# A 16-row, two-layer post-norm transformer in one kernel: first mixture and small attention one step earlier in the loop, routing at step 2, reciprocal roots of gathered rows once a group

## What is computed

```python
x = layernorm(x + attn0(x))   # RMS norm, 16 heads of 64, softmax over 256 keys
x = layernorm(x + moe0(x))    # router with bias, top 2 of 8 experts (128-256-128, gelu) + a shared expert
x = layernorm(x + attn1(x))   # per token: softmax over 16 "heads" of size 8, then a projection
x = layernorm(x + moe1(x))    # router, top 2 of 8 experts (128-512-128, gelu)
```

## Time and profile before

| | us |
|---|---|
| median of 3 runs | 1513.58 |
| lowest and highest run | 1510.7, 1517.77 |
| the profiled execution, its own time | 1511.41 |
| its span, first to last instruction | 1509.7 |

### The profile page before, as it was taken

How to read it: one execution, slowest core, us unless ns; L and a number is a source line. 1 busy time by engine, 2 the same in 40 slices (tenths; PEclk the granted TensorE clock), 3 DMA queues, 4 the chain that set the end, 5 groups by cost and what they waited for, 6 DMA issues and landing times.

```text
span 1509.7 us, 27533 instructions
## 1 busy us (share of the span) xinstructions
PE 1223.3 (81%) x9532; PEld 1040.3 (69%) x9532; DVE 942.9 (62%) x2405; ACT 833.6 (55%) x2405; POOL 579.5 (38%) x504
## 2 busy tenths in 40 slices
PE   6898969887978787878788887868787869999805
PEld 5776758675867676757575767657676748999805
DVE  4466676767766676766766767675776665721235
ACT  5775647565656565655656574645565554654401
POOL 3015151606060606151525242245646360513564
PEclk9998999899999999999989998999999988999957
DMA  4110000000000000000000000000000013999813
GB/s 137 76 69 5 1 5 2 4 1 5 1 5 1 1 5 1 5 1 5 1 5 1 5 1 5 1 5 29 4 22 2 22 38 123 339 337 349 274 35 106
DMA packets 50875, 76.64 MB, mean 51 GB/s; under 512 B 6058, under 2 KB 36147, under 8 KB 50739
## 3 DMA queue, kind: packets, MB, share of 16 engines
q1 hardware_dynamic: 46898, 67.02, 13.1%
q0 software_dynamic: 3840, 7.87, 1.7%
HBM read 58.75 MB, written 16.12 MB: 50 GB/s over the span
## 4 chain that ended last, share of the span: by engine, by line
issue 37%; DVE 17%; POOL 16%; ACT 13%; PE 11%; DVEq 3%; POOLq 2%; DMA 1%; SPq 0%; ACTq 0%
ACT probs L758 7%; POOL prod_buffer L645 5%; POOL values L671 3%; DVE score L1156 2%; DVEq L437 2%; POOL xs L660 2%; POOLq L437 2%; DVE neg_max L912 2%; POOL std_inv L601 2%; ACT probsT L737 2%; DVE score L1161 2%; DVE shifted L967 2%; PE bank_S L1398 2%; DVE x L956 1%; DVE prod_buffer L1131 1%
## 5 line engine op out<-in xcount | busy, mean ns | idle before, releaser
L758 ACT ACTIVATE probs<-bank_S,neg_max 128x256 f32<-128x256 f32 x512 | 235.9, 475 | 141.1 <-DVE neg_max L912 141.1
L912 DVE TENSOR_REDUCE neg_max<-bank_S 128x2 f32<-128x512 f32 x256 | 164.6, 684 | 112.4 <-PE bank_S L1398 111.2
L645 POOL TENSOR_TENSOR prod_buffer<-score,qkv 128x1024 f32<-128x1024 f32 x60 | 167.7, 2818 | 51.2 <-ACT score L774 51.2
L633 POOL TENSOR_TENSOR prod_buffer<-qkv 128x1024 f32<-128x1024 f32 x45 | 124.1, 2758 | 140.9 <-ACT qkv L737 140.9
L1457 PE MATMUL bank_A<-probsT,values 128*64 128x256 f32 x1024 | 150.1, 417 | 4.5 <-ACT probsT L737 3.2
L600 POOL TENSOR_TENSOR var_eps<-mv,ln_eps 128x2 f32<-128x2 f32 x48 | 9.5, 198 | 364.1 <-DVE mv L950 364.1
L1435 PE MATMUL bank_T<-ident,probs 128*128 128x128 f32 x1024 | 145.3, 285 | 1.8 <-ACT probs L758 0.6
L737 ACT ACTIVATE probsT<-bank_T 128x512 f32<-128x512 f32 x256 | 139.4, 604 | 8.8 <-PE bank_T L1435 8.8
L1435 PEld LDWEIGHTS bank_T<-ident,probs 128*128 128x128 f32 x1024 | 117.2, 145 | 36.9 <-issue 30.8
L1549 PE MATMUL bank_F<-down,hid 128*128 128x128 f32 x960 | 119.5, 281 | 4.5 <-DVE x L1014 3.5
L1549 PEld LDWEIGHTS bank_F<-down,hid 128*128 128x128 f32 x960 | 114.9, 198 | 7.9 <-DVE x L1014 6.5
(11 more groups left out here) (333 smaller groups left out, 3370.9 us busy)
## 6 DMA issues: line engine op xcount, KB each, us to landing
probs<-in_w SPq DMA_DIRECT2D x22, 512.0 KB, 5.4
oT<-in_w SPq DMA_DIRECT2D x21, 512.0 KB, 4.8
w_own<-in_w SPq DMA_DIRECT2D x19, 512.0 KB, 5.4
probsT<-in_w SPq DMA_DIRECT2D x11, 512.0 KB, 5.1
xb<-xs SPq DMA_DIRECT2D x36, 128.0 KB, 5.5
wo<-in_w SPq DMA_DIRECT2D x9, 512.0 KB, 5.6
xs<-hid SPq DMA_DIRECT2D x36, 128.0 KB, 5.5
xs<-w_own SPq DMA_DIRECT2D x1, 3072.0 KB, 9.6
```

The lines of the kernel that those rows point to most:

```text
L633: settled(pool, g.tensor_tensor(prod[:, t, half(i)], q, k, ALU.mult))
L645: g.tensor_tensor(pv1[:, t, half(i)], *weights_and_values(t, i), ALU.mult).then_inc(pv1_ready, 1)
L758: ins = sc.activation(probs[:, h // 2 % 2, h % 2, t, :], unit.bank(f"S{h}")[:, t * S:(t + 1) * S], ACT.Exp, bias=neg_max[:, h, t:t + 1], a ...
L912: ve.tensor_reduce(neg_max[:, h, :], v.bank(f"S{h}")[:, :].rearrange("p (t k) -> p t k", t=NT), AX.X, ALU.max, negate=True).then_inc(max_r ...
```

## The change

Four things are moved in the loop, and one in the tail. (1) The units of the first mixture, of the small attention and of the second routing stand one step or more earlier in PE's order; ACT's and DVE's parts follow: `mix(1)` and `mix(2)` in step 0, `mix(3)` and `first_out` in step 1, `ln_apply(1)` in step 2, the copies of LQ and `head_product` in step 3. `head_scores` and `head_exp` stay. (2) `second_norm` is in step 0, the copy of X3T in step 1, `second_route` in step 2; `map_blocks` and `input_norm` go to step 4. (3) QK0 takes a bank of the ring G instead of A, and `first_pair(1)` stands behind `first_route`. (4) `inverse_out` takes a group of rows: POOL gathers a group without roots between, waits for the statistics of the row whose buffer it takes, and makes the roots once for rows 0 to 9, once for rows 10 to 14, once for row 15; DVE applies them at the end of a group, for group 1 after the last `dense_mix` and the statistics of row 15.

```diff
--- before.py
+++ after.py
@@ -99,9 +99,9 @@
     return len([q for q in range(min(p + 1, SPARSE)) if q % RING == p % RING])
 
 
-FILL_B = {(0, 1): ["D0p2"], (1, 0): ["WT0"], (1, 1): ["D0p3"], (2, 0): ["D0base"], (3, 0): ["X2T"], (4, 0): ["LQ0", "LQ1"]}
-FILL_C = {(2, 1): ["X3T"], (5, 1): ["R1"]}
-FILL_MAP = {(2, 1): ["CN"]}
+FILL_B = {(0, 0): ["D0p2"], (0, 1): ["WT0", "D0p3"], (1, 1): ["D0base"], (2, 1): ["X2T"], (3, 0): ["LQ0", "LQ1"]}
+FILL_C = {(1, 0): ["X3T"], (2, 0): ["R1"]}
+FILL_MAP = {(3, 1): ["CN"]}
 BESIDE = {0: ["X3T"], 1: ["R1"], 2: ["RK"], 3: ["X2T"], 4: ["CN", "LQ0", "LQ1"], 13: ["AOT"], 14: ["PROJ"], 16: ["X3E"], 17: ["R1E"]}
 EXPS, GATE_EXPS = 8, (4, 19)
 
@@ -149,7 +149,7 @@
         put("A", "HT", on=nxt and s == HP - 2)
         put("F", *fill_units(it, s, 1))
     put("A", f"O{HP - 1}")
-    put("A", "QK0", on=nxt)
+    put("G", "QK0", on=nxt)
     put("G", "OUT")
     put("G", "RK", on=it >= 2)
     put("G", "V0", "V1", "V2", "V3", on=nxt)
@@ -671,11 +671,12 @@
                         g.indirect_dma_start(yg[:, row % YG_RING, t, c, :], None, xs[i].rearrange("b s d -> (b s) d"),
                                              bass.IndirectOffsetOnAxis(ap=slots_of[:, row, t, c:c + 1], axis=0)).then_inc(gathered[row % YG_RING], 16)
 
-            def inverse_out(row):
-
-                pool.wait_ge(out_stats_ready, row + 1)
-                settled(pool, g.tensor_tensor(var_out[:, row, :], mv_out[:, row, :, 1], ln_eps[:], ALU.add))
-                g.tensor_tensor(std_out[:, row, :], var_out[:, row, :], minus_half[:], ALU.pow).then_inc(out_std_ready, 1)
+            def inverse_out(rows):
+
+                pool.wait_ge(out_stats_ready, rows[-1] + 1)
+                whole = slice(rows[0], rows[-1] + 1)
+                settled(pool, g.tensor_tensor(var_out[:, whole, :], mv_out[:, whole, :, 1], ln_eps[:].rearrange("p (a t) -> p a t", a=1).broadcast_to([P, len(rows), NT]), ALU.add))
+                g.tensor_tensor(std_out[:, whole, :], var_out[:, whole, :], minus_half[:].rearrange("p (a t) -> p a t", a=1).broadcast_to([P, len(rows), NT]), ALU.pow).then_inc(out_std_ready, 1)
 
             def tail(v):
                 inverse_std(v, 1, 1)
@@ -683,12 +684,13 @@
                 for row in GROUPS[1]:
                     scatter(row)
                 inverse_std(v, 2, 1)
-                for row in range(ROWS - 1):
-                    gather(row)
-                    if row >= 2:
-                        inverse_out(row - 2)
-                for row in range(ROWS - 3, ROWS):
-                    inverse_out(row)
+                for rows in GROUPS:
+                    for row in rows:
+                        if row >= YG_RING:
+                            pool.wait_ge(out_stats_ready, row - YG_RING + 1)
+                        gather(row)
+                    inverse_out(rows)
+                inverse_out(range(ROWS - 1, ROWS))
 
             def body(v):
                 if v.it == ROWS:
@@ -854,23 +856,23 @@
                         transposed_probs(v, s)
                     if v.a and s + 1 < HP:
                         softmax_exp(v, 2 * s + 2)
-                    if v.b and s == 3:
-                        copy_out(v, "X2T", x2T[:], v.bank("X2T")[:, 0:S])
                     if v.a and s + 1 < HP:
                         softmax_exp(v, 2 * s + 3)
                     if v.a and s >= 1 and s != HP - 2:
                         o_out(v, s - 1)
+                    if v.b and s == 3:
+                        for t in range(NT):
+                            copy_out(v, f"LQ{t}", qkv1[:, t].rearrange("p h c d -> p (h c d)"), v.bank(f"LQ{t}")[:, 0:3 * D])
                     if v.a and s != HP - 2:
                         repeat_inverse(v, s)
-                    if v.b and s == 1:
+                    if v.b and s == 0:
                         copy_out(v, "WT0", gates0T, v.bank("WT0")[0:E + 1, 0:S])
                     if v.a and s != HP - 2:
                         transposed_probs(v, s)
                     if v.a and s + 3 < HP:
                         qk_out(v, s + 3)
-                    if v.b and s == 4:
-                        for t in range(NT):
-                            copy_out(v, f"LQ{t}", qkv1[:, t].rearrange("p h c d -> p (h c d)"), v.bank(f"LQ{t}")[:, 0:3 * D])
+                    if v.b and s == 2:
+                        copy_out(v, "X2T", x2T[:], v.bank("X2T")[:, 0:S])
                     if v.next and s == 1:
                         squares_of(v)
                     if v.b and s == 5:
@@ -1099,7 +1101,7 @@
                 dve.drain()
 
             def out_norm(row):
-                dve.wait_ge(out_std_ready, row + 1)
+                dve.wait_ge(out_std_ready, group_of(row) + 1 if row < ROWS - 1 else len(GROUPS) + 1)
                 for t in range(NT):
                     ins = ve.tensor_scalar(x3[:, row, t, :], x3[:, row, t, :], mv_out[:, row, t, 0:1], std_out[:, row, t:t + 1],
                                            ALU.subtract, ALU.mult)
@@ -1245,21 +1247,17 @@
                 second_gate(row)
                 for r in GROUPS[0]:
                     combine(r)
-                    if r >= 2:
-                        out_norm(r - 2)
-                for r in GROUPS[0][-2:]:
+                for r in GROUPS[0]:
                     out_norm(r)
                 dense_mix(v, 0)
                 dense_mix(v, 1)
                 for n, r in enumerate(GROUPS[1]):
                     dense_mix(v, n + 2)
                     combine(r)
-                    if n >= 2:
-                        out_norm(r - 2)
                 dense_mix(v, E - 1)
-                for r in GROUPS[1][-2:]:
+                out_stats(row)
+                for r in GROUPS[1]:
                     out_norm(r)
-                out_stats(row)
                 out_norm(row)
 
             def body(v):
@@ -1271,41 +1269,40 @@
                     mix(v, 0, False)
                 inverse_sums(v, 0)
                 for s in range(HP):
-                    if v.b and s == 3:
-                        ln_apply(1, x2[:], v.at(1, 1, 1))
                     if s + 1 < HP:
                         head_max(v, 2 * s + 2)
                         head_max(v, 2 * s + 3)
                     if s + 2 < HP:
                         lower_qk(v, s + 2)
                     if v.b and s == 0:
-                        mix(v, 1, False)
+                        mix(v, 1)
+                        mix(v, 2, False)
                     if v.b and s == 1:
-                        mix(v, 2, False)
-                    if v.b and s == 2:
                         mix(v, 3)
                     if s >= 1:
                         o_scale(v, s - 1)
+                    if v.c and s == 0:
+                        second_norm(v.it - 2)
+                    if v.c and s == 1:
+                        transposed_out(v, "X3T", x3T[:])
                     if v.b and s == 2:
-                        first_out(v)
+                        ln_apply(1, x2[:], v.at(1, 1, 1))
                     if s + 1 < HP:
                         inverse_sums(v, s + 1)
-                    if v.c and s == 1:
-                        second_norm(v.it - 2)
-                    if s == 2 and v.it in MAP_ITERATION:
+                    if v.b and s == 1:
+                        first_out(v)
+                    if v.b and s == 3:
+                        head_product(v)
+                    if v.c and s == 2:
+                        second_route(v, "R1", v.it - 2)
+                    if s == 4 and v.it in MAP_ITERATION:
                         map_blocks(v)
-                    if v.c and s == 3:
-                        transposed_out(v, "X3T", x3T[:])
-                    if v.next and s == 3:
+                    if v.next and s == 4:
                         input_norm(v)
                     if v.next and s == HP - 2:
                         input_transposed(v)
-                    if v.b and s == 4:
-                        head_product(v)
                     if v.b and s == 5:
                         head_scores(v, 0)
-                    if v.c and s == HP - 2:
-                        second_route(v, "R1", v.it - 2)
                     if v.b and s == HP - 1:
                         head_scores(v, 1)
                 o_scale(v, HP - 1)
@@ -1320,12 +1317,12 @@
                     place_row(v, v.it - 2)
                 ln_apply(0, x1[:], v.at(0, 1, 1))
                 transposed_out(v, "X1T", None, x1T)
-                if v.next:
-                    first_pair(v, 1)
                 if v.b:
                     head_softmax_sum(v, 0)
                     head_out(v, 0)
                 first_route(v)
+                if v.next:
+                    first_pair(v, 1)
                 if v.b:
                     head_softmax_sum(v, 1)
                     head_out(v, 1)
```

## The result

The changed kernel takes **1490.97 us** (median of 4 runs, 1490.47 to 1491.35) against 1514.04 us of the kernel before in the same session (4 runs, 1510.7 to 1517.77): ratio 0.9847, 95% interval 0.9823 to 0.987. So it is faster by 1.5%, and the forecast of 1443 us with its range of 1420 to 1480 us is missed by 48 us.

What follows compares the result with a forecast made beforehand. No engine is full; chains of waits set the end. From the profiled 1511.4 us, loop -36 and tail -35, plus 2.2 to the median of the runs: 1442.6, rounded to 1443 us, range 1420 to 1480.

Steps and rivals of the forecast that it cites:

- loop sum: Loop: -4.1 + 1.5 at head_scores(1), ln_apply(0) 2.4 us earlier; -36 us over 15 iterations.
- net cost at the input transpose: Loop, end of the earlier mixture's lateness: 1.5 us late, bounds 0 (all given back) and 2.9 (nothing).
- Part 3: Loop, small attention earlier: POOL's head products start about 4 us earlier; input_norm beside them waits 1.1 us, bounds 0 and 2.8.
- Part 2: Loop, mixture one step forward: step-1 scores 2.9 us late, partly given back after step 3, net cost 1.5 us.
- Part 1: Loop, second_route moved from step 6 to step 2 on DVE: gain of 4.1 us before o_scale(6).
- the hole: Loop, DVE's stretch from the end of hT_lo to o_scale(6), holding second_route: 4.1 us, longer than the work.
- Part 4: Loop end, QK0 into ring G: OUT follows o_scale(6) on PE, takes 3.6 to 4.57 us; gain 0.3, bounds 0 and 1.0.
- Part 5: Tail, grouped roots on POOL: gathers at 5.08 us a row, first root pair 3.0 us; gain 35 us, bounds 28 and 38.
- (a): Rival: loop gives nothing, lateness and held input_norm use up second_route's gain; only the tail gains, 1478.6 us; chance 0.20.
- (c): Rival: tail gathers stay at 7.5 us a row, the DMA queue's pace; tail gives some 10 us, 1467.6 us; chance 0.10.
- (d): Rival: step 0's order delays step 1, nothing given back; loop loses 4.8 us an iteration, 1550.6 us; chance 0.05.
- What would show it: Signs in loop and tail: 76 us between residuals, gathers every 5.1 us; a 78 us period or 7.5 us pitch refutes.

Runs made afterwards that it cites:

- e5_both: Changed kernel with input_norm ahead of POOL's head products and POOL's first product waiting for both LQ copies: 1524.99 us against 1567.81 of the kernel before, ratio 0.9729.
- e7_oldtail: Kernel of e5_both, but with the tail of the kernel before: 1465.06 us where the kernel before takes 1515.11, ratio 0.9667.
- e9_late: Kernel of e5_both with only the second routing put back to step 6, behind the input transpose: 1451.24 us against 1515.11 of the kernel before, ratio 0.9571.
- cured loop: Loop of e5_both, the changed loop with both edits against held DVE instructions: 75.1 us between residuals, where the changed loop has 79.2.
- a2_after: The changed kernel itself, run again on another chip where the kernel before takes 1567.81 us: 1586.81 us, ratio 1.0134.
- e5c_both: Same kernel as e5_both, run once more where the kernel before takes 1569.17 us: 1527.08 us, ratio 0.9762.
- the first run: The changed kernel as first timed and profiled: 1490.97 us against 1514.04 of the kernel before, ratio 0.9847.

## Why the prediction was wrong

The forecast's execution was 1511.4 - 36 - 35 = 1440.4 us, the profiled one took 1490.5: 50 us apart. The part ahead of the tail accounts for 36 + 8.5 = 44.5 of them, the tail for 35 - 29.5 = 5.5. The term of the loop sum that failed is the net cost at the input transpose: 1.5 us within bounds of 0 and 2.9, measured 5.0. With it the gain of 4.1 us is gone. Two instructions that POOL holds make the difference; without them the cost is 0.9.

- **Part 3 is the step that failed.** It foresaw the collision of `input_norm` with POOL's products and priced it at 1.1 us within bounds of 2.8; it is 3.53 - 0.47 = 3.05 us. Its argument was that the wait ends with one POOL product and that the next `head_max` has slack for a part; in the trace the two instructions wait for a sum and then a product, and the `head_max` follows without a gap. The Trainium skill (SBUF — State Buffer, § Who interferes with whom), which Part 3 set aside as not shown, says that a `tensor_scalar` in a two-port mode and a GpSimd instruction shut each other out for a whole instruction; here the first of the two starts at 666.31 and 1.2 us later POOL's sum of 666.17 ends (667.45), the second ends with the product of 667.41 (669.76), and the trace agrees. The second collision was not foreseen at all: Part 2 put DVE's `head_product` "into a place where DVE waits anyhow", at no cost. It is held for 3.27 - 1.23 = 2.04 us. In the earlier trace rows DVE had begun it at 655.60, 0.05 us ahead of POOL's at 655.65, and POOL had paid (3.39 us). In the changed order ACT's copy of LQ0 lets POOL go before DVE is free. The same section of the Trainium skill says that the one that issues first gets the ports; 3.27 and 2.36 us in the one order, 1.23 and 3.18 in the other (e5_both) agree. Together 5.1 us, each directly ahead of a `head_max`: the +4.8 us of iteration 1. Without them the mean over all 15 iterations is 75.4 us (e7_oldtail) where 76.0 was forecast.
- **Part 1** was right that `shifted` was held and that the hole had 4.1 us, and wrong in whom it credited. e9_late gives the routing's own move 0.8 us an iteration. The effects of the two moves don't add up: with the small attention earlier the collision is gone, with the routing in step 2 and in step 6 alike. The sum also counted 15 iterations, and iteration 1 has no second routing and no hole.
- **Part 2's** 2.9 us (3.3 measured) at step 1 was right. That half of it is given back by the input transpose was wrong in the changed kernel, but right, even too careful, in the cured loop, with 0.9 us left.
- **Part 4**: OUT takes 3.73 us at a granted clock of 1.00 (684.2 to 687.9), as its lower bound of 3.6 said. The working missed that OUT waits for `o_scale(6)` and `o_scale(7)` only in front of its last matmuls; it begins at 684.23, 0.7 us ahead of the end of `o_scale(7)`. That changed no sign.
- **Part 5** had the right mechanism. Gathers at 5.06 us a row against 5.08; row 9's statistics 55.3 us behind the first gather against 55.5; norms 5.21 against 5.6. Mis-sized is the root pair: 7.2 us and not 3.0. That it is nearly the upper bound is luck: the bound was ten times the power of 2 columns, and the power takes 3.55 us, the drain ahead of it 3.42 though nothing is in flight. The second pair, 1.78 + 1.99 us, had no term; `dense_mix(7)` and the statistics of row 15, 1.6 us in the sum, run beside it, and so does row 15's own root beside the norms. The 4.2 us of the first pair and about 2 of the second, with small gains elsewhere, make the 5.5.
- **The rivals.** (a), the loop gives nothing, was the nearest with 1478.6, and its reason names `input_norm` held; it lacked the head product and thus a loss. (c) is refuted, the gathers keep their pace. (d) came true for iteration 1 alone, and by another mechanism; that its 4.8 us are met to the digit is chance. That the tail could turn against the kernel on another chip stood nowhere.
- **What would show it** expected `input_norm` over 0.5 us, `shifted` near 0.2 and the step-1 scores 2 to 3 us late, and all came; so none of them tells the forecast from a loss. The period of 78 us, its sign of being wrong, came too: 79.2.

## What to carry to other kernels

When work of one engine moves beside a long instruction of another that can hold it, here DVE's beside POOL's, list every instruction in the new neighbourhood and ask who starts first; a two-input instruction that was harmless by 0.05 us is a term of the sum. A cure by order (one more wait on POOL, one call moved up) was worth more here than the change itself: 1586.8 us became 1525.0 on one chip. A gain from taking waits out of a queue of DMAs should be measured on more than one chip: here the waits were what let the other engines go on.

## What the runs showed that was not expected

- **A drain on POOL has a price for each indirect DMA issued since the last one, even when all have landed**: 0.15 us behind none, 0.47 behind 4, 1.14 behind 12, 1.47 behind 16, 1.78 behind 20, 3.42 behind 40, so 0.15 us and about 0.08 for each. Behind 4 gathers just issued it is 1.6 to 4.7 us in the kernel before.
- **A power on POOL costs by the column**: 0.70 us for 2, 1.99 for 10, 3.55 for 20, so about 0.16 us a column beyond a fixed 0.4. The plain addition ahead of it takes 0.20 to 0.21 us for any of them.
- **Indirect DMAs in a row can slow the other engines to a crawl.** On one kind of chip 40 of them without a drain left 52 GB/s and 3 matmuls in 10 us. In a2_after PE's records stand 2.8 us apart, each put down to no wait that the profile shows:

```profile
1462.26 0.37 PE L1531 MATMUL bank_S<-probs,hidb 128*128 128x128 f32 x1 [2.44 <-issue]
1465.06 0.37 PE L1531 MATMUL bank_S<-probs,hidb 128*128 128x128 f32 x1 [2.43 <-issue]
```

  DVE too stands still between instructions of one routine (e5c_both), which follow each other without a gap in the first run:

```profile
1400.96 0.61 DVE L1091 SCALAR_TENSOR_TENSOR x<-values,gates_of,x 128x128 f32<-128x128 f32 x2 [2.55 <-issue]
1403.76 0.61 DVE L1091 SCALAR_TENSOR_TENSOR x<-values,gates_of,x 128x128 f32<-128x128 f32 x2 [2.19 <-issue]
```

  It needs no other transfers. In the loop POOL issues 16 scatters in a row while nearly nothing else is moved. Windows of 10 us in them, first a2_after, then the same kernel in the first run:

```profile
1044.00:1054.00 10.00, 3.85 (x14) 1.56 (x12) 0.00 (x0) 1.81 (x4) 7.60 (x8) 0.66 0.16 52
```

```profile
1044.00:1054.00 10.00, 9.78 (x84) 7.43 (x84) 6.68 (x18) 5.50 (x22) 7.56 (x9) 1.00 0.16 53
```

  The scatters move the same 52 to 53 GB/s; PE executes 14 matmuls on the one chip and 84 on the other. In a2_after DVE starts at 1056.6 on the maxima of scores that PE ended by 1044.2. So starved transfers of weights are not the whole cause. A drain behind each row's gathers avoids it. What holds the other engines' instructions, and why only on that kind of chip, stays open.
